# A two-level Strassen product for pairs of row groups in the hidden layers of a gated MLP

## What is computed

```python
xn = layernorm(x)                                    # x: 16384 x 1024, fp32
s = attn(xn)            # exp random features of xn times those of a weight matrix
h = silu((xn @ w1.T) * w1_s) * ((xn @ w2.T) * w2_s)   # 1024 -> 4096
h = gelu((h @ h1.T) * h1_s)                           # 4096 -> 4096
h = gelu((h @ h2.T) * h2_s)                           # 4096 -> 4096
g = silu((h @ w3.T) * w3_s)                           # 4096 -> 1024
y = x + s * g
```

## Time and profile before

| what | value |
|---|---|
| runs (us) | 2350.95, 2351.78, 2828.28 |
| median | 2351.78 us |
| profiled execution | 2350.2 us, span 2349.2 us |
| cores, from the first to the last instruction | 2346.5 to 2349.2 us |
| mean granted TensorE clock of the cores | 0.997 to 0.998 |
| TensorE, VectorE, ScalarE, GpSimd busy | 99%, 50%, 19%, 10% |
| HBM read, written | 415.31 MB, 29.36 MB |

### The profile page before, as it was taken

The page is one execution under the profiler, slowest core; times in us unless marked ns, Lnnn a source line. Parts: engine busy times, 40 slices in busy tenths (PEclk is TensorE's granted clock), DMA queues, the critical chain, the costliest instruction groups (busy, mean ns, idle before and its releaser), DMA issues.

```text
span 2349.2 us, 30063 instructions; the slowest of 8 cores (2346.5 to 2349.2 us)
## 1 busy us (share of the span) xinstructions
PE 2327.1 (99%) x10744; PEld 1051.5 (45%) x10744; DVE 1170.5 (50%) x1394; ACT 438.9 (19%) x620; POOL 228.6 (10%) x393
## 2 busy tenths in 40 slices
PE   7999999999999999999999999999999999999998
PEld 3444444444444444444444444444444444444443
DVE  4677543434644343463664777534334543433465
ACT  3222111111111111111623222111111111111111
POOL 1000000000000000012040000000000000000000
PEclk9999999999999999999999999999999999999999
DMA  7656566665856566598533555565656756565698
GB/s 113 111 83 88 79 107 95 96 107 89 157 92 108 95 96 106 89 195 134 103 108 94 85 77 86 89 109 84 108 92 103 153 94 109 84 110 90 104 196 202
DMA packets 92306, 253.69 MB, mean 108 GB/s; under 512 B 9856, under 2 KB 28416, under 8 KB 91904
## 3 DMA queue, kind: packets, MB, share of 16 engines
q0 software_dynamic: 57168, 192.96, 55.0%
q1 hardware_dynamic: 34992, 58.81, 8.3%
HBM read 415.31 MB, written 29.36 MB: 189 GB/s over the span
## 4 chain that ended last, share of the span: by engine, by line
PE 94%; DVE 4%; DMA 1%; issue 1%; ACT 0%; DVEq 0%; POOL 0%; ACTq 0%; POOLq 0%
PE pb L160 92%; PE pb L377 1%; DVE blk L342 1%; DMA wring<-w3p 1%; DMA blk<-xT 0%; DVE blk L323 0%; DVE blk L327 0%; DVE blk L324 0%; DVE blk L326 0%; DVE blk L325 0%; PE pb L239 0%; PE pb L240 0%; DVE blk L273 0%; DVE blk L267 0%; DVEq L125 0%
## 5 line engine op out<-in xcount | busy, mean ns | idle before, releaser
L160 PE MATMUL pb<-blk,wring 128*128 128x512 bf16 x9904 | 2139.5, 379 | 2.6 <-DVE blk L342 1.7
L160 PEld LDWEIGHTS pb<-blk,wring 128*128 128x128 bf16 x9904 | 968.2, 98 | 1173.4 <-issue 7.9
L486 DVE TENSOR_TENSOR wring<-wring 128x2048 bf16<-128x2048 bf16 x216 | 264.8, 1226 | 223.9 <-PE pb L160 167.4
L553 DVE TENSOR_TENSOR tmp<-pb,tmp 128x512 f32<-128x512 f32 x72 | 49.8, 692 | 366.5 <-PE pb L160 365.6
L493 DVE TENSOR_TENSOR wring<-wring 128x2048 bf16<-128x2048 bf16 x144 | 176.4, 1225 | 15.4 <-DVE blk L659 0.5
L609 ACT ACTIVATE blk<-tmp,cols 128x512 bf16<-128x512 f32 x128 | 92.6, 724 | 399.4 <-DVE tmp L553 227.6
L609 ACT ACTIVATE blk<-pb,cols 128x512 bf16<-128x512 f32 x64 | 44.1, 689 | 606.6 <-PE pb L160 606.6
L160 PE MATMUL pb<-blk 128*128 128x512 bf16 x640 | 138.6, 379 | 0.0
L189 POOL DMA_DIRECT2D wring<-h1p x128 | 67.6, 528 | 708.6 <-PE pb L160 708.0
L189 POOL DMA_DIRECT2D wring<-h2p x128 | 67.7, 529 | 705.9 <-PE pb L160 684.2
L531 DVE TENSOR_TENSOR tmp<-pb,tmp 128x512 f32<-128x512 f32 x72 | 49.8, 692 | 167.5 <-PE pb L160 166.3
(11 more groups left out here) (85 smaller groups left out, 650.7 us busy)
## 6 DMA issues: line engine op xcount, KB each, us to landing
wring<-h1p POOLq DMA_DIRECT2D x128, 512.0 KB, 7.4
wring<-h2p POOLq DMA_DIRECT2D x128, 512.0 KB, 7.5
wring<-w12p POOLq DMA_DIRECT2D x64, 512.0 KB, 9.0
wring<-w3p POOLq DMA_DIRECT2D x32, 512.0 KB, 10.4
blk<-xT SPq DMA_DIRECT2D x32, 256.0 KB, 7.7
y<-blk SPq DMA_DIRECT2D x32, 256.0 KB, 4.1
blk<-xT POOLq DMA_DIRECT2D x16, 256.0 KB, 20.5
s_hbm<-blk SPq DMA_DIRECT2D x16, 256.0 KB, 2.1
```

Of the source, the lines that this page charges most:

```text
L160: ii = t.matmul(p[bk], lhs, rhs, start=(not onto and i == 0), stop=(i == n - 1), skip_group_check=onto)
L486: tok = V(lambda: v.tensor_add(wring[:, so, :], wring[:, slots[ka][0], :], wring[:, slots[kb][0], :]), *toks, slots[ka][1], slots[kb][1])
L553: a = V(lambda: v.tensor_add(tb, p[bb], ta), m, vv, t_free.get(2 * par + 1))
```

## The change

In the stages h1 and h2, groups 0 to 11 form six pairs (0 and 1, 2 and 3, ...). `in_pair` gives 0 for the even one, 1 for the odd one, and None elsewhere (groups 12 to 15 and w3). The even group runs no M1 and makes no s1 in `wring`. `pair_first` adds its a11 and a22 into a buffer x of four tiles. The odd group makes its own s1 in `wring`. In place of its M1 it runs `pair_product`: the product of the two groups' s1 (256 rows x 2048) with the M1 operand (2048 x 512) by a second 2 x 2 Strassen scheme, seven units of 8 matmuls of 256 columns. Its weight operands are half-width sums and differences of x and y_ (the odd group's s1): w5 behind `pair_first`, w2 and w1 behind unit M2, and two differences in place behind M5, the last of which is the token `w_tok`. Its five activation operands are made once in a stage (`pair_operands`, behind M4 of group 0). The results join the two groups' `tmp` tiles: those of the even group hold M7 and M6 joined with a subtraction and wait (`held`) for the pair product, which then emits outputs 11 and 22 of the even group. The in-place differences a12-a22 and a21-a11 of the odd group come behind the product.

The buffers of the second scheme lie in tiles 6 to 15 of the output blocks of the running stage. So that they are free, outputs 11, 22 and 21 of groups 4 to 11 are written to tile 4 or 5 (`place`) and from there to HBM (`park`). Behind the units of group 12 `bring_back` loads them into their tiles (`edge_12`). The sums of the last edges wait for these loads.

```diff
-                ii = t.matmul(p[bk], lhs, rhs, start=(not onto and i == 0), stop=(i == n - 1),
-                              skip_group_check=onto)
+                ii = t.matmul(p[bk][:, 0:width], lhs, rhs, start=(not onto and i == 0),
+                              stop=(i == n - 1), skip_group_check=onto)
...
+        def pair_operands(l2, bl, *toks):
+            op = blk[:, bl["M1"], :].rearrange("p (k c) -> p k c", c=N)
+            b11, b12 = op[:, 0:8, 0:N2], op[:, 0:8, N2:N]
+            b21, b22 = op[:, 8:16, 0:N2], op[:, 8:16, N2:N]
+            l2["M2"], l2["M5"] = b11, b22
+            for q, fn, x, y_ in (("M1", v.tensor_add, b11, b22), ("M4", v.tensor_sub, b21, b11),
+                                 ("M3", v.tensor_sub, b12, b22), ("M7", v.tensor_add, b21, b22),
+                                 ("M6", v.tensor_add, b11, b12)):
+                l2["ready"] = V(lambda: fn(l2[q], x, y_), *toks)
+
+        def pair_first(s_, nm, r, l2):
+            x = l2["x"]
+            a = V(lambda: v.tensor_add(x, wring[:, slots[s_, nm, r, "a11"][0], :],
+                                       wring[:, slots[s_, nm, r, "a22"][0], :]),
+                  l2.get("last"), slots[s_, nm, r, "a11"][1], slots[s_, nm, r, "a22"][1], *l2["toks"])
+            l2["s5"] = V(lambda: v.tensor_add(l2["w5"], x[:, 0:1024], x[:, 1024:2048]))
+            return a
+
+        def pair_product(s_, nm, r, bl, l2, u_tok, emit):
+            t0, tok0 = 2 * ((r - 1) % 2), held.pop(r - 1)
+            t1 = 2 * (r % 2)
+            u2 = tmp[:, t1 + 1, 0:N2]
+            lo0, hi0 = tmp[:, t0:t0 + 2, 0:N2], tmp[:, t0:t0 + 2, N2:N]
+            lo1, hi1 = tmp[:, t1, 0:N2], tmp[:, t1, N2:N]
...
+            def unit2(bk, op, onto=False):
+                need(t, l2["ready"], l2["s5"], l2["w_tok"])
+                return mm_group(bk, [(w[op][:, k * 128:(k + 1) * 128], l2[op][:, k, :])
+                                     for k in range(8)], onto, width=N2)
...
+            m = unit2(bb, "M2")
+            c_tok = S(lambda: sc.copy(u2, pv(bb)), m, t_free.get(t1 + 1))
+            m = unit2(ba, "M5")
+            r_tok = V(lambda: v.tensor_add(u2, pv(ba), u2), m, c_tok)
+            m = unit2(bc, "M1")
+            a = V(lambda: v.tensor_sub(u2, pv(bc), u2), m)
+            free_bank(bc, a)
+            need(t, c_tok)
+            m = unit2(bb, "M4", onto=True)
+            q21 = V(lambda: v.tensor_sub(lo1, pv(bb), lo1), m, u_tok)
+            need(t, r_tok)
+            m = unit2(ba, "M3", onto=True)
+            q12 = V(lambda: v.tensor_add(hi0, both(pv(ba)), hi0), m, tok0)
+            need(t, q21)
+            m7 = unit2(bb, "M7", onto=True)
+            need(t, q12)
+            m6 = unit2(ba, "M6", onto=True)
+            V(lambda: v.tensor_add(lo0, both(u2), lo0))
+            V(lambda: v.tensor_sub(hi1, hi1, u2))
+            a = V(lambda: v.tensor_add(lo0, both(pv(bb)), lo0), m7)
+            free_bank(bb, a)
+            t_free[t0 + 1] = emit("11", r - 1, tmp[:, t0 + 1, :], a)
+            t_free[t0] = emit("22", r - 1, tmp[:, t0, :], a)
+            a = V(lambda: v.tensor_sub(hi1, pv(ba), hi1), m6)
...
-            sub_in_place(s_, nm, r, "a12", "a22", slots[key("s5")][1])
+            if part != 1:
+                sub_12()
+            else:
+                x, y_ = l2["x"], wring[:, slots[key("s1")][0], :]
+                V(lambda: v.tensor_add(l2["w2"], y_[:, 0:1024], y_[:, 1024:2048]),
+                  l2.get("last"), slots[key("s1")][1])
+                V(lambda: v.tensor_add(l2["w1"], x[:, 0:1024], y_[:, 1024:2048]))
             edge_(0, m)
...
             m = unit(ba, "s5", "M5")
             give_slot(key("s5"), m)
-            sub_in_place(s_, nm, r, "a21", "a11", slots[key("s2")][1])
+            if part != 1:
+                sub_21()
             rr = V(lambda: v.tensor_add(ta, p[ba], ta), m, a)
+            if part == 1:
+                V(lambda: v.tensor_sub(x[:, 1024:2048], x[:, 1024:2048], y_[:, 1024:2048]))
+                l2["w_tok"] = V(lambda: v.tensor_sub(y_[:, 0:1024], y_[:, 0:1024], x[:, 0:1024]))
             edge_(1, m)
...
+            elif part == 0:
+                x_tok = pair_first(s_, nm, r, l2)
+                vv = None
+            else:
+                m, vv = pair_product(s_, nm, r, bl, l2, rr, emit)
+                give_slot(key("s1"), m)
+                sub_12()
+                sub_21()
             edge_(2, m)
...
+            def bring_back(q, ks):
+                need(sy, read_tok[11], l2["last"], *[now(d_park[q, i]) for i in range(2)])
+                back[q] = d_back[q].inc(
+                    sy.dma_start(blk[:, bl["out" + q], ks.start * N:ks.stop * N]
+                                 .rearrange("p (k c) -> p k c", c=N),
+                                 park[s_, nm, q][:, ks.start - 4:ks.stop - 4, :]), 16)
...
                     a = S(lambda: sc.activation(dst, src, AF.Gelu, scale=s_col[:, oc:oc + 1]),
-                          tok, *first_tok)
+                          tok, *first_tok,
+                          *([now(d_park[q, r % 2]), read_tok.get(r - 2)] if parked else []))
+                    if parked:
+                        need(sy, a)
+                        d_park[q, r % 2].inc(sy.dma_start(park[s_, nm, q][:, r - 4, :], dst), 16)
```

More of the change, by code:

```diff
@@ L107, in build_nc @@
         d_rel = {op: Ctr(nc, stack, f"d_rel{op}") for op in ("M3", "M6")}
+        d_park = {(q, i): Ctr(nc, stack, f"d_park{q}{i}") for q in ("11", "22", "21") for i in range(2)}
+        d_back = {q: Ctr(nc, stack, f"d_back{q}") for q in ("11", "22", "21")}
         d_xn = Ctr(nc, stack, "d_xn")
@@ L151, in free_bank, with mm_group @@
             banks.append((i, tok))
-        def mm_group(bk, pairs, onto=False, late_ops={}):
+        def mm_group(bk, pairs, onto=False, late_ops={}, width=N):
             n = len(pairs)
@@ L176, in build_nc @@
                     for q in ("s2", "s5", "s1"):
-                        plan.append(("S", (s_, nm, r, q), None))
+                        if not (q == "s1" and in_pair(nm, r) == 0):
+                            plan.append(("S", (s_, nm, r, q), None))
         plan = deque(plan)
@@ L502, in edge_ @@
                     fn()
+            part = in_pair(nm, r)
             par = r % 2
@@ L511, in unit, with sub_12, sub_21 @@
                                 onto, ops_ready.get(op, {}))
+            def sub_12():
+                sub_in_place(s_, nm, r, "a12", "a22", slots[key("s5")][1])
+            def sub_21():
+                sub_in_place(s_, nm, r, "a21", "a11", slots[key("s2")][1])
             bb = take_bank()
@@ L537, in row_group @@
             m = unit(bb, "a22", "M4", onto=True)
-            give_slot(key("a22"), m, slots[key("a12")][1])
+            give_slot(key("a22"), m, slots[key("a12")][1], x_tok)
             out21 = emit("21", r, p[bb], m)
+            if part == 0 and r == 0:
+                pair_operands(l2, bl, *l2["toks"])
             edge_(3, m)
@@ L548, in row_group @@
             edge_(4, m)
+            join = v.tensor_sub if part == 0 else v.tensor_add
             need(t, out21)
@@ L552, in row_group @@
             give_slot(key("a12"), m)
[L553 removed]
+            a = V(lambda: join(tb, p[bb], ta), m, vv, t_free.get(2 * par + 1))
             free_bank(bb, a)
[L555 removed]
+            if part != 0:
+                t_free[2 * par + 1] = emit("11", r, tb, a)
             if nxt:
@@ L562, in row_group @@
             give_slot(key("a21"), m)
-            a = V(lambda: v.tensor_add(ta, p[ba], ta), m)
+            a = V(lambda: join(ta, p[ba], ta), m)
             free_bank(ba, a)
-            t_free[2 * par] = emit("22", r, ta, a)
-            if nxt:
+            if part != 0:
+                t_free[2 * par] = emit("22", r, ta, a)
+            else:
+                held[r] = a
+            if nxt and in_pair(nxt[1], nxt[2]) != 0:
                 weight_sums(*nxt, "s1")
@@ L579, in hidden_stage, with place, edge_12 @@
             reload_tok = {}
+            read_tok = {}
+            back = {}
+            def place(r):
+                return 4 + r % 2 if 4 <= r < 12 else r
+            def bring_back(q, ks):
[4 more added lines that the diff above has]
+                                 park[s_, nm, q][:, ks.start - 4:ks.stop - 4, :]), 16)
+            def edge_12(u, m):
+                if 1 <= u <= 3:
+                    bring_back(("11", "22", "21")[u - 1], slice(6, 12))
+                elif u >= 4:
+                    bring_back(("11", "22", "21")[u - 4], slice(4, 6))
             def sums_out(r):
                 i = 2 * (r % 2)
-                a = V(lambda: v.tensor_sub(stg[:, i + 1, :], stg[:, i, :], kt(o22, r)),
+                a = V(lambda: v.tensor_sub(stg[:, i + 1, :], stg[:, i, :], kt(o22, place(r))),
                       o_tok["12", r], o_tok["22", r], now(d_stg[i + 1]))
@@ L618, in emit @@
                     if r < 14:
-                        late[0] = [lambda: sums_out(r)]
```

(1 more changed line is left out.)

57 lines of the change are left out of this document (42 added, 15 removed).

## The result

The changed kernel takes 2430.4 us (median of 4 runs, 2429.5 to 2431.8) against 2351.8 us before: ratio 1.034, 95% interval 1.032 to 1.035. It is slower by 79 us. The forecast was 2433 us.

A forecast was written before the change was run, and what follows sets the result against it. The kernel was taken to run at the speed of TensorE's matmul columns. Against 2350.2 us, -18.0 + 66.4 + 5.3 + 3.7 + 24.0 = +81.4 gave 2431.6; the median lies 1.6 higher, so 2433 us, range 2421 to 2443.

The forecast's parts named there:

- The wait: After M5 of every odd group, TensorE waits for rr and two weight differences: 2.77 us lost, 24 times, +66.4 us.
- The columns: M1 of 24 pairs becomes 56 matmuls of 256 columns at 0.110 us (upper end 0.125): -18.0 us.
- Inside the product: M6 of the pair product waits for q12 to read bank ba: 0.22 us, 24 times, +5.3 us.
- The clock: TensorE's granted clock falls behind 0.6 of the 24 product waits, 1.67 us each: +24.0 us, ends 0 and +40.1.
- Rival A: The clock falls after every product wait: 2449 us, chance 0.20.
- Rival B: The clock never falls after the product waits: 2409 us, chance 0.17.
- Start of a stage: M3 of group 0 waits for a late rr, 1.14 or 0.72 us, twice each: +3.7 us (0 to 8).
- The reload: Loading parked outputs back at group 12 is covered: nothing, or a few us if it delays weights.
- The operand sums: Five sums after rr in group 0, 5 x 1.33 us, costed at nothing; uncovered, up to 1 us, 4 times.
- Rival C: Not slower by 2%: the wait for w_tok is shorter than stepped, 2384 us at its lower end; chance 0.08.
- rival D: 256-column matmuls take 0.125 us and the reload of group 12 delays weights: 2463 us, chance 0.08.
- The time without the wait: Without the wait after M5, the change would gain only 18 - 9 us.

The follow-up runs named there:

- Experiment 1: The changed kernel with the two half-width weight differences issued ahead of rr, nothing else changed: 2348.8 us, ratio to before 0.9989.
- experiment 3: The kernel before, with s1's two halves rewritten behind rr in odd groups of h1 and h2 and M1 waiting for them, no pair product: 2427.5 us, ratio 1.0325.
- experiment 5: Experiment 1 plus another unit order in the pair product, M1 and M7 between M3 and M6: 2344.0 us, ratio 0.9977.

## Why the prediction was right

**The wait.** The seven steps from the last matmul of M5 to the first of the product gave 2.60 us of idle time and 24 waits; the trace has 2.60 and 2.61, 24 times. Experiment 1 takes it away by order alone, experiment 3 puts it into the kernel before: both move the time by what was forecast. The steps came from the rows of single operations, and none of them was an average over stages.

**The columns.** 0.109 us a matmul, against 0.110 taken; the upper end of 0.125 wasn't needed. The rule of the Trainium skill (TensorE: Matmul & The Clock Gate, section "Back-to-back issue gap") gives 109 ns, and the trace agrees: 0.1088. The section gives that rule for a matmul by itself, and about 131 ns for one of 512 columns in a stream with weight loads; the stream here takes 216 ns, so the measurement goes with the rule and against that figure.

**Inside the product.** 0.23 us against 0.22; experiment 5 confirms that it is bank ba between M3 and M6.

**The clock.** The mechanism was right, and the number was a choice between bounds: 0.6 of 24 at 1.67 us taken, 13 of 24 at 1.55 us measured on the slowest core, 24.0 against 20.2 us; over all eight cores it was 89 of 192. The trace before could have said more than the one row that was read the earlier trace rows: all eight cores have the idle time of 2.32 us in the head, and on five of them the clock fell behind it. Rival A, a fall behind every wait, which is where the Trainium skill (TensorE: Matmul & The Clock Gate, section "A second HAM failure mode: psum-queue depth-cycling") pointed, didn't happen at 2.61 us nor at 3.40; the trace agrees with it only in that the clock swings and each fall is paid for. Rival B, no fall, is what a wait of 1.81 us does. The share isn't a property of the length alone: the same 2.61 us gave 9 to 13 falls of 24 where the waits lay 50.6 us apart (52.0 behind a fall), and 2 to 7 where they lay 51.1 apart. What sets it was not settled. So the forecast of this term was partly luck, and the total is closer than its terms because the columns (-1.6 us) and the clock (-3.8) erred against the stage starts (+2.1) and what was not foreseen (+1.7).

**Start of a stage.** This term was mis-sized, 3.7 against 5.8 us. The step that failed: "One weight sum less (1.23 + 0.10) brings rr's end to 641.54". The timeline where h1 ends and h2 begins, with the last join, the Gelu behind it, the sum that waits for it, rr and M3's start:

```profile
650.85 0.69 DVE L677 TENSOR_TENSOR tmp<-pb,tmp 128x512 f32<-128x512 f32 x1 [0.52 <-PE pb L166]
...
651.63 0.72 ACT L748 ACTIVATE blk<-tmp,cols 128x512 bf16<-128x512 f32 x1 [1.96 <-DVE tmp L677]
652.46 0.42 DVE L796 TENSOR_TENSOR blk<-blk 128x512 bf16<-128x512 bf16 x1 [0.92 <-ACT blk L748]
...
661.90 0.69 DVE L621 TENSOR_TENSOR tmp<-pb,tmp 128x512 f32<-128x512 f32 x1 [0.24 <-ACT blk L748]
...
663.05 7.07 PE L166 MATMUL pb<-blk,wring 128*128 128x512 bf16 x32 [1.95 <-DVE tmp L621]
```

The sum at 652.46 waits for the end of the Gelu at 652.35. In the kernel before, the weight sum that is gone (L486) stood in that time, beside the Gelu:

```profile
630.47 0.69 DVE L563 TENSOR_TENSOR tmp<-pb,tmp 128x512 f32<-128x512 f32 x1 [0.72 <-PE pb L160]
631.26 0.72 ACT L609 ACTIVATE blk<-tmp,cols 128x512 bf16<-128x512 f32 x1 [2.16 <-DVE tmp L563]
631.27 1.23 DVE L486 TENSOR_TENSOR wring<-wring 128x2048 bf16<-128x2048 bf16 x1
```

Without it VectorE waits instead, and from the join to rr it takes 11.05 us where it took 11.71 (630.47 to 642.18), 0.66 us less and not 1.33. M3 then starts 0.46 us after rr has ended, where the prediction had 0.15; that rest is unexplained.

**Left out.** The reload was called covered "or a few us". In the change it cost one short wait on the slowest core; with the long waits gone it costs 0.4 to 1.0 us of idle time in each stage on the slowest core (experiment 1). The operand sums were put at nothing; there they showed as waits for `w_tok` of 1.7 us in all. Rival C (a shorter wait) and rival D (0.125 us a matmul) did not occur. The time without the wait was put at a gain of 18 - 9 us; experiment 1 gained 2.4 (2348.8 us against 2351.2 measured beside it), since the operand sums and the reload, covered by the waits, then showed.

## What to carry to other kernels

Where one engine is busy 99% of the time, read a change by the order of the instructions on the engines that feed it: what is ready early must not be issued behind what becomes ready last, and here three instructions in the wrong order cost four times what the arithmetic saved. Price such a wait from the start of the last matmul to the start of the next, step by step, and then ask what the idle time does to the clock. A wait that is taken away uncovers the smaller ones behind it, so look for these before promising the whole gain.

## What was not expected of the hardware

The granted clock did not fall behind any of 192 waits of 1.81 us, and fell behind 15 to 20 of 24 waits of 3.40 us on each core. One that fell cost 1.2 to 1.8 us whatever the width of the matmuls, and 2.7 to 2.9 us behind five of the waits of 3.40 us. At 2.61 us the count differed between cores that ran the same instructions (9 to 13 of 24), and what the falls cost differed by 6.7 us between the core with the shortest span and the one with the longest, whose spans are 6.5 us apart. There a core whose clock had fallen behind one wait mostly kept it through the next (6 falls in 75); at 3.40 us it did not (93 in 112).
